# A vision layer on one core: a new order of the per-image step, and the last eleven expert tiles added straight into the output

## The reference, cut to what matters

```python
# x: (16, 4, 128, 256); 16 images, 4 groups, 128 tokens, 256 features
w   = softmax_over_groups(gelu(mean(x.sum(1), -1) @ w1.T + b1) @ w2.T + b2)
h   = einsum('bgcd,gbc->bcd', x, w)                       # token selection
h   = h + attention(layernorm(h))                         # 16 heads of 16, relative bias, softmax, Wo
n   = layernorm(h)
g   = softmax(n @ Wg + bg), kept for its two largest of 8 experts, divided by their sum
out = h + sum_e g[e] * (gelu(n @ W1[e] + b1[e]) @ W2[e] + b2[e])   # hidden width 1024
```

## Time and profile before

| | before |
|---|---|
| median of 3 runs | 532.65 us (532.6 to 533.27) |
| the profiled execution | 531.54 us, its span 529.5 us |
| PE / PEld busy | 480.4 / 408.0 us |
| ACT / DVE / POOL busy | 261.7 / 219.0 / 178.2 us |
| PE's share of the chain that ended last | 71% |

### The profile page before, as it was taken

How to read it: one execution, slowest core, us unless ns; L and a number is a source line. 1 busy time by engine, 2 the same in 40 slices (tenths; PEclk the granted TensorE clock), 3 DMA queues, 4 the chain that set the end, 5 groups by cost and what they waited for, 6 DMA issues and landing times.

```text
span 529.5 us, 13085 instructions
## 1 busy us (share of the span) xinstructions
PE 480.4 (91%) x3742; PEld 408.0 (77%) x3743; DVE 219.0 (41%) x1068; ACT 261.7 (49%) x1003; POOL 178.2 (34%) x186
## 2 busy tenths in 40 slices
PE   3779989999999998699999999999999999999970
PEld 2457756676767675499999899999999999999960
DVE  2575788887888887422331111111111111111110
ACT  1247799889998888734323322233322333222310
POOL 3011123223334633313266533333332333333321
PEclk9889999999999999989999999999999999999995
DMA  8792030313213036287576556666667666677415
GB/s 269 220 351 72 22 101 22 102 40 102 77 46 101 22 103 183 60 295 191 181 196 158 161 183 196 193 162 164 184 194 198 178 161 171 184 197 187 123 20 168
DMA packets 51004, 78.61 MB, mean 148 GB/s; under 512 B 10528, under 2 KB 39472, under 8 KB 50768
## 3 DMA queue, kind: packets, MB, share of 16 engines
q1 hardware_dynamic: 40160, 66.80, 39.1%
q0 software_dynamic: 8592, 10.58, 11.8%
q10 hardware_dynamic: 2208, 0.71, 0.6%
HBM read 68.27 MB, written 11.90 MB: 151 GB/s over the span
## 4 chain that ended last, share of the span: by engine, by line
PE 71%; issue 10%; DVE 7%; ACT 5%; DMA 3%; POOL 3%; POOLq 0%; DVEq 0%; SPq 0%; ACTq 0%
PE psVO L959 24%; PE psS L947 13%; PE psP L947 13%; PE psQK L786 4%; PE psP L819 4%; PE psS L809 3%; ACT prob L592 3%; DVE prob L1126 2%; PE psVO L797 2%; PE psVO L844 2%; PE psQK L935 2%; DMA fold<-xn_dram,sel 1%; PE psG L865 1%; PE psCX L833 1%; POOL meta_dram L445 1%
## 5 line engine op out<-in xcount | busy, mean ns | idle before, releaser
L959 PE MATMUL psVO<-xw,prob 128*128 x624 | 141.7, 380 | 0.8 <-DVE fold L1348 0.8
L959 PEld LDWEIGHTS psVO<-xw,prob 128*128 128x128 f32 x624 | 115.5, 190 | 15.7 <-issue 1.2
L491 POOL DMA_INDIRECT sum_dram<-fold,sel x39 | 62.0, 1590 | 163.4 <-DMA sel<-meta_dram 112.3
L592 ACT ACTIVATE prob<-prob,smin 128x128 f32<-128x128 f32 x256 | 99.9, 400 | 4.7 <-DVE smin L1126 4.4
L679 ACT ACTIVATE prob<-psS,b1T 128x128 f32<-128x128 f32 x160 | 45.6, 368 | 94.3 <-PE psS L947 94.3
L679 ACT ACTIVATE prob<-psP,b1T 128x128 f32<-128x128 f32 x152 | 43.3, 368 | 92.5 <-PE psP L947 92.5
L947 PEld LDWEIGHTS psS<-fold,w1c 128*128 128x128 f32 x640 | 76.0, 195 | 1.7 <-DVE fold L1343 0.9
L947 PE MATMUL psS<-fold,w1c 128*128 128x128 f32 x640 | 76.5, 279 | 0.6 <-DVE fold L1343 0.6
L947 PEld LDWEIGHTS psP<-fold,w1c 128*128 128x128 f32 x608 | 70.8, 192 | 0.9
L947 PE MATMUL psP<-fold,w1c 128*128 128x128 f32 x608 | 71.0, 275 | 0.0
L434 POOL TENSOR_TENSOR rstd<-ve,minus_half 128x1 f32<-128x1 f32 x32 | 23.8, 743 | 135.2 <-DVE ve L1089 133.3
(11 more groups left out here) (166 smaller groups left out, 490.0 us busy)
## 6 DMA issues: line engine op xcount, KB each, us to landing
w1c<-in_L_ffn_W SPq DMA_DIRECT2D x39, 1024.0 KB
xw<-in_x SPq DMA_DIRECT2D x16, 512.0 KB, 7.8
xw<-in_L_ffn_W SPq DMA_DIRECT2D x8, 1024.0 KB, 6.5
sum_dram<-h_all SPq DMA_DIRECT2D x17, 128.0 KB
xn_dram<-xn SPq DMA_DIRECT2D x16, 128.0 KB, 1.7
out<-sum_dram SPq DMA_DIRECT2D x4, 512.0 KB, 5.7
relb<-in_L_ffn_b SPq DMA_DIRECT2D x1, 1024.0 KB, 7.9
sel<-meta_dram SPq DMA_DIRECT2D x39, 2.0 KB
```

The source lines that it names most:

```text
L491: pool.indirect_dma_start(out=sum_dram.ap()[0:EARLY_B * S if j < EARLY else N_TOK + P, :], out_offset=bass.IndirectOffsetOnAxis(ap=row_no[ ...
L592: i = act.activation(blk, blk, ACT.Exp, bias=smin[:, k:k + 1], scale=-1.0, accum_out=ssum[:, k:k + 1])
L959: i = pe.matmul(psVO[:, 0:D], hT[u][:, c * P:(c + 1) * P], xw2[:, bass.ds(e * (HC * D) + c * D, D)], start=(c == 0), stop=(c == HC - 1))
```

## The change

It has two parts.

**The image step.** The queues of PE, ACT and DVE get a new order. On ACT `qk_evac` comes before the third group of exponentials, `exp(i, u, 0)` goes between the fourth group of image i-1 and the last two `pT_evac`, and `x1T_evac` comes before `x2T_evac`. On PE `scores(i, 0)` comes right behind `project_v` (and `ranks`), and `scores(i, 1)` before `turn_x`, `turn_xn2`, `values(i-1, 1)`. On DVE the statistics of the first norm become `first_stats`, behind `mask_keys`; `biased(i, 0)` comes right behind `residual`, `biased(i, 1)` behind `spread`, both norms and `rows` behind these, and `normalise` to the end.

**The last tiles.** The 25 late tiles are divided into 14 (MID) and 11 (LAST); the eleven are tiles that are full whatever the routing is, so that they have no padding rows. Two tables are computed in place of one. SP copies `sum_dram` to `out` once the scatter of tile 27 has landed, in its queue between the weight loads of tiles 31 and 32; scatters 28 to 38 add into `out` and the first of them waits for the copy. POOL leaves out a scatter at j = 31 and is one tile further behind from there on. `yout` becomes two buffers; each scatter now waits on POOL for the one before.

```diff
+LAST = -(-(SLOTS - E * (P - 1)) // P) - EARLY
+MID = TILES - EARLY - LAST
...
-        yout = fold[:, 3 * D:4 * D]
+        yout = [fold[:, 3 * D:4 * D], sel[:, 0:D]]
...
+            with sp.Fori(EARLY // 2, (EARLY + MID) // 2 + 2) as t:
+                for u in range(2):
+                    next_records(2 * t + (u + 1))
+                    load_w1(2 * t + u, u)
+            out_v = out.rearrange("b p d -> (b p) d")
+            rows_ = N_TOK // 4
+            sp.wait_ge(y_scat, 16 * (EARLY + MID))
+            for i in range(4):
+                sp.dma_start(out_v[i * rows_:(i + 1) * rows_, :],
+                             sum_dram.ap()[i * rows_:(i + 1) * rows_, :]).then_inc(fin_out, 16)
+            with sp.Fori((EARLY + MID) // 2 + 2, TILES // 2) as t:
                 for u in range(2):
                     next_records(2 * t + (u + 1))
                     load_w1(2 * t + u, u)
             load_w1(TILES - 1, 0)
+            sp.wait_ge(fin_out, 16 * 4)
             sp.wait_ge(y_scat, 16 * TILES)
-            out_v = out.rearrange("b p d -> (b p) d")
-            rows_ = N_TOK // 4
-            for i in range(4):
-                sp.dma_start(out_v[i * rows_:(i + 1) * rows_, :],
-                             sum_dram.ap()[i * rows_:(i + 1) * rows_, :]).then_inc(fin_out, 16)
-            sp.wait_ge(fin_out, 16 * 4)
...
             def scatter(j):
 
                 pool.wait_ge(y_sb, j + 2)
+                if j > 0:
+                    pool.wait_ge(y_scat, 16 * j)
+                if j == EARLY + MID:
+                    pool.wait_ge(fin_out, 16 * 4)
                 own_wait(pool)
                 pool.indirect_dma_start(
-                    out=sum_dram.ap()[0:EARLY_B * S if j < EARLY else N_TOK + P, :],
+                    out=sum_dram.ap()[0:EARLY_B * S if j < EARLY else N_TOK + P, :] if j < EARLY + MID
+                    else out.rearrange("b p d -> (b p) d"),
...
                 gather(j)
-                scatter(j - 3)
+                if j < EARLY + MID + 3:
+                    scatter(j - 3)
+                elif j > EARLY + MID + 3:
+                    scatter(j - 4)
...
             def step(i, u, front=True, back=True, late=True, nxt=True, batch=None, tanh=False, ahead=True):
-                if back:
-                    exp(i - 1, 1 - u, 2)
                 if front:
                     qk_evac(i)
                 if back:
+                    exp(i - 1, 1 - u, 2)
                     pT_evac(i - 1, 0)
                     pT_evac(i - 1, 1)
                     exp(i - 1, 1 - u, 3)
...
+                if front:
+                    exp(i, u, 0)
                 if back:
                     pT_evac(i - 1, 2)
                     pT_evac(i - 1, 3)
-                if back:
                     r_evac(i - 1)
                 if ahead:
                     first_group(i + 2)
-                if front:
-                    exp(i, u, 0)
+                if nxt:
+                    x1T_evac(i + 1)
                 if late:
                     x2T_evac(i - 2)
-                if nxt:
-                    x1T_evac(i + 1)
                 if front:
                     exp(i, u, 1)
                     v_evac(i)
...
+                if front:
+                    scores(i, 0)
                 if back:
                     values(i - 1, 0)
                     context(i - 1, 1 - u, 2)
-                if front:
-                    scores(i, 0)
-                if back:
                     context(i - 1, 1 - u, 3)
                     spread_sums(i - 1)
+                if front:
+                    scores(i, 1)
+                if nxt:
+                    turn_x(i + 1)
                 if late:
                     turn_xn2(i - 2, batch)
-                if nxt:
-                    turn_x(i + 1)
                 if back:
                     values(i - 1, 1)
-                if front:
-                    scores(i, 1)
...
                 if front:
                     mask_keys(dve, i, 0)
+                if nxt:
+                    first_stats(i + 1)
                 if late:
                     residual(i - 2)
+                if front:
+                    biased(i, u, 0)
                 if back:
                     reciprocals(i - 1, 1 - u)
                     spread(i - 1)
+                if front:
+                    biased(i, u, 1)
                 if nxt:
                     first_norm(i + 1)
+                if late:
+                    second_norm(i - 2)
                 if place is not None:
                     rows(place)
-                if late:
-                    second_norm(i - 2)
                 if gate is not None:
                     masks(gate)
-                if front:
-                    biased(i, u, 0)
-                    biased(i, u, 1)
...
-                if back:
-                    normalise(i - 1)
                 if front:
                     biased(i, u, 2)
                     biased(i, u, 3)
+                if back:
+                    normalise(i - 1)
                 if late:
                     keep_logits(i - 2)
...
-            def result(j, e):
+            def result(j, u, e):
                 dve.wait_ge(y_ps, j + 2)
                 dve.wait_ge(y_sb, j + 1)
                 dve.tensor_tensor(ysum, psVO[:, 0:D], relb[:, bass.ds(e * D, D)], ALU.add).then_inc(y_step, 1)
                 dve.wait_ge(y_step, j + 2)
-                if not (isinstance(j, int) and j == 0):
-                    dve.wait_ge(y_scat, 16 * j)
-                dve.tensor_scalar(yout, ysum, metas[:, bass.ds(j * META + 1, 1)], None, ALU.mult) \
+                if not (isinstance(j, int) and j <= 1):
+                    dve.wait_ge(y_scat, 16 * (j - 1))
+                dve.tensor_scalar(yout[u], ysum, metas[:, bass.ds(j * META + 1, 1)], None, ALU.mult) \
                     .then_inc(y_sb, 1)
...
-            tile_table(EARLY, LATE, P - 1, True)
-            dve.wait_ge(tables_ok, 2)
+            late_counts()
             xs_evac(6)
-            result(4, expert(4))
+            result(4, 0, expert(4))
+            middle_table()
             xs_evac(7)
-            result(5, expert(5))
+            result(5, 1, expert(5))
+            last_table()
+            dve.wait_ge(tables_ok, 3)
             xs_evac(8)
```

More of the change, by code:

```diff
@@ L172, in vit_layer_kernel @@
         row_no = metas.bitcast(I32)
-        c_ge, c_gt = (fold[0:1, 1280 + i * LATE * E:1280 + (i + 1) * LATE * E] for i in range(2))
-        at = 1280 + 2 * LATE * E
+        at = 1280
+        c_ge, c_gt = (fold[0:1, at + i * TABLE * E:at + (i + 1) * TABLE * E] for i in range(2))
+        at += 2 * TABLE * E
         c_w, incl = (fold[0:1, at + i * E * E:at + (i + 1) * E * E] for i in range(2))
[L176 to L179, removed]
+        at += 2 * E * E
+        c_e, c_off, c_in, tile_no = (fold[0:1, at + i * TABLE:at + (i + 1) * TABLE] for i in range(4))
+        at += 4 * TABLE
+        c_step, c_room, c_all, c_last, taken_step = (fold[0:1, at + i * E:at + (i + 1) * E] for i in range(5))
+        at += 5 * E
+        taken, taken_too = (fold[0:1, at + i * (E + 1):at + (i + 1) * (E + 1)] for i in range(2))
         psS = [ps("psS0"), ps("psS1")]
@@ L369, in _ @@
             load_w1(EARLY - 2, 0)
-            sp.wait_ge(tables_ok, 2)
+            sp.wait_ge(tables_ok, 3)
             sp.wait_ge(scat, 16 * TOPK * B)
@@ L1270, in _ @@
             select_groups(0)
+            first_stats(0)
             first_norm(0)
@@ L1319, in tile_table @@
                 then(dve.tensor_tensor(c_in[:, 0:tiles], tile_no[:, 0:tiles], c_off[:, 0:tiles], ALU.add))
-                if late:
-                    then(dve.tensor_scalar(c_in[:, 0:tiles], c_in[:, 0:tiles], taken[:, 0:1], float(E * ROW_TILES),
+                if first is not None:
+                    then(dve.tensor_scalar(c_in[:, 0:tiles], c_in[:, 0:tiles], first[:, 0:1], float(E * ROW_TILES),
                                            ALU.add, ALU.min))
-                dve.tensor_scalar(tile_row[:, at:at + tiles], c_in[:, 0:tiles], float(P), None, ALU.mult) \
-                    .then_inc(tables_ok, 1)
@@ L1326, in tiles_taken @@
-            def tiles_taken():
-                then(dve.tensor_tensor(c_room[:, :], c_t[:, :], c_end[:, :], ALU.subtract))
-                then(dve.tensor_scalar(c_room[:, :], c_room[:, :], float(EARLY), 0.0, ALU.add, ALU.max))
-                then(dve.tensor_tensor(taken[:, 0:E], c_room[:, :], c_t[:, :], ALU.min))
-                then(dve.tensor_tensor(taken_step[:, :], taken[:, 1:E + 1], taken[:, 0:E], ALU.subtract))
-            dve.wait_ge(gp_late, 4)
-            tile_table(0, EARLY, 0, False)
+                then(dve.tensor_scalar(tile_row[:, at:at + tiles], c_in[:, 0:tiles], float(P), None, ALU.mult))
@@ new lines, in tiles_taken, with early_tables, late_counts @@
+            def tiles_taken(dst, src, tiles):
+                then(dve.tensor_tensor(c_room[:, :], src, c_end[:, :], ALU.subtract))
```

(58 more changed lines are left out.)

33 lines of the change are left out of this document (18 added, 15 removed).

## The result

Before: 531.27 us median (529.72 to 534.23, 20 runs). After: 534.9 us median (531.63 to 541.35, 20 runs). Ratio 1.0057, interval [1.0039, 1.0076]: 0.57% slower, or 3.6 us by the medians; the ratio leaves out one of after's 20 runs that was in a slow state. I had forecast 529.6 us and faster. The profiled execution of after has a span of 533.3 us where that of before has 529.5, so the two profiles differ by 3.8 us, nearly what the medians do.

What follows compares the result with a forecast made beforehand. It saw three limits: the image step's loop of waits, PE in the expert stage, and the final scatter and copy. Tiles' start +5.8, copy +0.8 and end -9.6 gave -3.0 us: 529.6 us, range 523.5 to 533.5.

Steps and rivals of the forecast that it cites:

- The end: After the last tiles: without the copy the span ends when the last scatter lands (3.80 us after issue); -9.6 us together.
- 0.3 us for the scaling that waited: Last scatter, part of the end's term: freed of the scaling behind the scatter before, it gains some 0.3 us.
- The image step: Ordinary steps: loops over ACT and PE make a step 11.55 us instead of 11.16, +0.4 each.
- Steps 0 to 3: First steps: step 2's selection logits cost +0.4 + 0.5, steps 1 and 3 lose about 1.1 together.
- The chain to the tiles: Between image steps and tiles: record pairs' waits absorb part of the 2.9 us move of `rows`; tiles start +5.8 us.
- The copy: Mid-stage, between weight loads of tiles 31 and 32: PE stalls 0 to 3 us before tile 32's hidden layer, taken as 0.8.
- The rivals: Not slower in the image step, 0.18; rigid chain or long stall, no change, 0.12; slower by the step's loop, 0.10.
- Slower by the step's loop: Image step, `project_v` to `gate_logits`: at 11.9 us a step 534.3 us, deciding from about 11.8; chance 0.10.

Runs made afterwards that it cites:

- the third order: Changed kernel, tail kept, image step reordered by summing the loop (projections right behind `project_qk`, gate logits last): 526.52 us, ratio 0.9897; repeated on another chip 526.61 us.
- the kernel with two orders: Kernel of the third order, but with the step order of before in steps 0 to 3: 536.93 us; unchanged on another chip 523.84 us, ratio 0.9851.

## Why the prediction was wrong

**The end: this step failed.** "The end then is the landing of the last scatter" took the landing (3.80 us) for the end, but the end is POOL's own, 8.8 us after it issues its last indirect DMA, to 0.01 us the same in the eight traces with nothing longer behind it. The page of before does not show it, since the copy covered it, but two other views do. The chain that ended last in before, whose last rows the prediction read, does not end in the copy but in POOL's queue, and the view of that line gives its length (start us, us, what; then count, ns least/median/most, starts):

```profile
511.42 3.80 DMA sum_dram<-fold,sel
...
516.26 1.77 POOLq L73
```

```profile
L73 POOLq DRAIN  x1: 8790/8790/8790, 516.3 to 516.3; - x1
```

The window from 525.3 to 529.50 is all that was there to win, 4.2 us. The other part of the term, 0.3 us for the scaling that waited, had the wrong sign: the last scatter is issued 1.1 us later after PE's end than in before. With the scatter of tile `j - 4` behind the gather of tile `j` from there on, five scatters are left behind the last gather instead of four, and each waits for the one before. The first of them was late besides: the prediction took 3.80 us for the landing of every scatter, but those into `out` in mid-stage took 6.2 to 8.0 us, and tile 34's scatter, at 506.12, waited for tile 33's, issued at 497.31, which took 8.0. How late the last one goes depends on that: in the run with `project_v` early, in which two of these landings took 4.0 us and POOL caught up, it was issued 1.8 us after PE's end and not 3.4. Together the end is -4.2 + 1.1 = -3.1 instead of -9.6. With that term alone put right the sum of the prediction is +3.5 us, and +3.6 were measured. That they are so close is luck: the interval alone is 2 us wide, and the errors of the other terms happen to cancel.

**The image step: right in mechanism, mis-sized.** The step was to be 11.55 and is 11.77. The exponentials start 0.19 us later than summed, nearly all of it because the statistics up to the first `biased` take 1.62 instead of 1.45 us (the wait of 0.74 at ScalarE is its wait for this whole path, not a cost of handing over); 0.03 more were lost between `x2T_evac` and the gate's logits. Over the steps from 4 to 15: the ordinary ones cost +0.61 each instead of +0.4, those with the gates' work and the placing steps 0.3 to 0.7 us each, so +5.6 where I had +3.2.

**Steps 0 to 3: over-sized, and hidden.** I had +2.0, and step 4 starts 0.3 us later. The cost is there: steps 1 to 3 take 38.29 us where they took 37.12, +1.2 (38.26 in the run with the new steps alone). But step 1 starts at 36.99 in after and at 37.86 in before. In the nine traces whose steps 0 to 3 have the old or the changed order, or one of these with `project_v` early, step 4 starts between 73.75 and 75.29, and the set-up and step 0 in front of these vary by more than the order costs (step 1 starts between 35.70 and 37.86). The 51.7 us of the third order's first profile have to be read with the same care: its later trace, with a start of step 4 at 75.17, has the same median.

**The chain to the tiles: right.** The pairs of records were to wait less for each other, and the part of the move of `rows` that is left is the +0.6 that I had (5.8 - 5.2): POOL's pair waits are 3.64 and 1.89 us where they were 4.55 and 4.37. Between two later traces, of the new steps alone and of the new tail alone, the same stretch differs by 0.5 (22.74 and 22.24).

**The copy: 0 instead of 0.8.** The lower bound of the stall, 0, held, though not by its reason, "the loads overlap as they do now": tile 32's weights did wait for the copy, some 2 us, and were in nearly 3 us before they were needed. The one wait for a gather behind it that the trace shows is of 0.42 us, at 505.57. A rule of the Trainium skill that I had weighed ("DMA: Bandwidth & Descriptors", "Queues, rings and completion order", descriptors of one row in ring order) agrees with this trace: the load of tile 32 was issued 5.2 us behind the copy's issue (454.60 against 449.44), and its first packet moved at 457.90, as the copy's last ones began. The same holds in the other traces with the new tail; in the last one of the kernel with two orders the copy's packets started from 440.56 to 446.05 and the first of the load behind it at 446.09. What the rule did not cost here is time of PE.

**The rivals.** "Slower by the step's loop" decided at 11.8 us a step by a sum that counted on the 9.6 of the end. The step stayed under it (11.77), and the kernel is slower all the same, for a reason that no rival held: all of them took 9.6 us from the end.

## What to carry to other kernels

Work that is taken off the very end uncovers what it lay over: before a final transfer is costed at its full length, ask when each engine's own queue would come to an end without it, and take from a run with that transfer cut short what is left. A loop of waits over several engines gets its length from the order as a whole; the same edit gave 0.4 us a step in one order and cost 0.8 in another, and a sum of the instructions along the loop, made for all engines at once, came within 0.05 us of the latter (11.9, 11.93) and of the order made from it (10.8, 10.81). What it gives is the step: the time of the whole kernel missed its forecast by 5 us with the same order. A variant that runs far off its sum in one place should be run on another chip before a mechanism is sought in it.

## What the hardware showed that I had not expected

- In these kernels POOL ends 8.8 us after it issues its last indirect DMA (8.79 to 8.80 in eight traces), although its data has moved long before: in after the share of the DMA engines is 0.00 from 528.0 to the end at 533.3.
- The landing of a scatter depends on what it meets. In after, in the stretch from 470 to 503, where a scatter is issued about 0.6 us ahead of a 1 MB weight load (468.48 and 469.09), a landing took 6.2 us at least, 6.5 in the median and 8.0 at most; in before, with 1.9 us between them (468.38 and 470.29), 3.8, 3.8 and 3.9. That the former go into `out` and the latter into `sum_dram` is not the reason: the last five into `out`, with no load behind them, took 3.7 to 3.9, and in the run with `project_v` early one into `out` took 4.0 with its load 2.8 us behind (469.38 and 472.20) and one took 6.5 with its load 0.5 us behind (478.98 and 479.44).
- On one chip, in one kernel, semaphores of the values' matmuls came 1.54 to 2.64 us after the matmul's start instead of 0.32, nine times, in the steps in which POOL issued indirect DMAs; the same program on another chip had none. The cause stays open.
